# Layer 0 attention: the value product in three rounded products, with rings of three for keys, values and split weights

## The reference

```python
x = x + tanh(g_xattn[0]) * L0_xattn(layernorm(x), ctx, Wq, Wk, Wv, Wo)      # the change is here
x = x + tanh(g_ffn[0])   * L0_ffn(layernorm(x), ...)
x = x + tanh(g_xattn[1]) * L1_xattn(layernorm(x), ctx, ...)
x = x + tanh(g_ffn[1])   * L1_ffn(layernorm(x), ...)
```

```python
hidden = concatenate([context, latents], axis=1)
q, k, v = latents @ Wq.T, hidden @ Wk.T, hidden @ Wv.T
attn = softmax(q @ k.T / sqrt(96))          # per head, 100 x 461
out  = attn @ v                             # 100 x 96 per head: "the value product"
return out @ Wo.T
```

## Time and profile before

| what | value |
|---|---|
| median of 3 runs | 2783.17 us (2781.26 to 2789.91) |
| the profiled execution | 2777.63 us, span 2775.8 us |
| PE busy | 2517.4 us, 91% of the span |
| DVE / ACT / POOL busy | 52% / 30% / 19% |
| mean granted clock of TensorE | 0.949 |
| attention of layer 0 | from about 843 to 1337 us of the span |

### The profile page before, as it was taken

One profiled execution on the slowest core, in us unless ns is written; L12 is line 12 of the kernel. 1 busy time (PEld: TensorE's weight loads), 2 busy tenths in 40 slices (PEclk: granted clock), 3 DMA queues, 4 the chain that ended last, 5 costly groups with the idle time before them and its releaser, 6 DMA issues. The chain is left out here.

```text
span 2775.8 us, 32483 instructions
## 1 busy us (share of the span) xinstructions
PE 2517.4 (91%) x12384; PEld 2109.7 (76%) x12384; DVE 1455.6 (52%) x2473; ACT 827.3 (30%) x1922; POOL 533.8 (19%) x414
## 2 busy tenths in 40 slices
PE   8999999799996899998769689999999999998824
PEld 6888888589995677776569468888888888886723
DVE  6222222223102576667543546666666766766697
ACT  3222222223212333333210234333333333332323
POOL 3000000000002122211021143334334334331120
PEclk9999999899997999999989889999999999999766
DMA  6222222253222222222021113323323223322001
GB/s 197 69 69 69 69 69 62 74 173 105 68 90 85 62 79 88 80 70 61 12 69 39 55 58 95 103 84 102 101 85 103 95 90 103 93 78 75 9 0 48
DMA packets 159357, 217.40 MB, mean 78 GB/s; under 512 B 31511, under 2 KB 124083, under 8 KB 158179
## 3 DMA queue, kind: packets, MB, share of 16 engines
q1 hardware_dynamic: 159202, 215.33, 25.4%
HBM read 176.99 MB, written 38.29 MB: 78 GB/s over the span
## 5 line engine op out<-in xcount | busy, mean ns | idle before, releaser
L1034 POOL TENSOR_TENSOR attend_w_hi<-attend_w_raw,attend_one 128x1024 fp32r<-128x1024 f32 (+1 forms) x184 | 335.9, 1840 | 478.6 <-DMA attend_w_raw<-in_wo 284.6
L1326 PE MATMUL attend_ps_score<-attend_k_in,attend_q 128*100 128x361 f32 (+1 forms) x768 | 298.1, 512 | 18.6 <-ACT attend_p L1078 11.0
L1271 PE MATMUL attend_ps_gemm<-normed_hi,attend_w_hi 128*128 128x400 f32 x704 | 268.3, 381 | 39.0 <-DVE attend_w_lo L1156 39.0
L1271 PE MATMUL attend_ps_gemm<-attend_o_hi,attend_w_hi 128*128 128x400 f32 x704 | 274.0, 389 | 27.0 <-DVE attend_w_lo L1156 24.5
L1156 DVE TENSOR_TENSOR attend_w_lo<-attend_w_raw,attend_w_hi 128x1024 fp32r<-128x1024 f32 (+1 forms) x184 | 216.7, 1212 | 155.8 <-POOL attend_w_hi L1034 154.8
L1081 ACT ACTIVATE attend_p<-attend_p,attend_neg_max 100x361 f32<-100x361 f32 x256 | 150.8, 590 | 398.0 <-DVE attend_neg_max L1181 398.0
L1271 PE MATMUL attend_ps_gemm<-attend_o_hi,attend_w_lo 128*128 128x400 f32 x704 | 244.7, 348 | 0.0
L1271 PE MATMUL attend_ps_gemm<-normed_lo,attend_w_hi 128*128 128x400 f32 x704 | 244.4, 347 | 0.0
L1271 PE MATMUL attend_ps_gemm<-attend_o_lo,attend_w_hi 128*128 128x400 f32 x704 | 244.2, 347 | 0.0
L1271 PE MATMUL attend_ps_gemm<-normed_hi,attend_w_lo 128*128 128x400 f32 x704 | 243.5, 346 | 0.0
L1211 DVE SCALAR_TENSOR_TENSOR stream_tokens<-attend_ps_gemm,attend_gate,stream_tokens 128x400 f32<-128x400 f32 x192 | 121.4, 633 | 230.3 <-PE attend_ps_gemm L1271 229.7
(11 more groups left out here) (252 smaller groups left out, 5071.4 us busy)
## 6 DMA issues: line engine op xcount, KB each, us to landing
attend_w_raw<-in_wq SPq DMA_DIRECT2D x88, 512.0 KB, 3.8
attend_w_raw<-in_wo SPq DMA_DIRECT2D x64, 512.0 KB, 5.1
attend_w_raw<-in_wo SPq DMA_DIRECT2D x32, 384.0 KB, 3.5
context_ctx_raw<-in_ctxT SPq DMA_DIRECT2D x8, 1456.0 KB
attend_k_in<-scratch_k SPq DMA_DIRECT2D x64, 180.5 KB
context_ctx_raw<-in_ctxF SPq DMA_DIRECT2D x22, 512.0 KB
scratch_v<-context_v_out SPq DMA_DIRECT2D x44, 256.0 KB, 2.2
scratch_k<-context_kt_out SPq DMA_DIRECT2D x44, 256.0 KB, 5.0
```

The lines of the kernel that those rows point to most:

```text
L1034: pool.tensor_tensor(hi, w_flat(w_raw, j % RAW, j), one[:hi.shape[0]].to_broadcast(hi.shape), ALU.mult).then_inc(w_hi_done, 1)
L1271: mm = pe.matmul(out, left[a](c), right[b](c), start=(c == 0 and a == b == 0), stop=(c == chunks - 1 and a == 1))
L1326: pe.matmul(ps_score[:S, h % 2, :NK], q[:, i % 2, h, k * S:(k + 1) * S], k_in[:, u % KV_SLOTS], start=True, stop=True).then_inc(s_done, 1)
```

## The change

In layer 0 the value product is computed as three rounded products. For that `v_hi` and `v_lo` are made by GpSimd, `pt_hi` by ScalarE from `ps_turn`, and `pt_lo` by VectorE from `ps_turn` and `pt_hi`, for all four chunks. The rings of keys and values and of split weights have three buffers in layer 0 in place of four (3 + layer). Layer 1 is as before.

```diff
-    RAW, SPLIT = 3, 4
-    P_SLOTS, KV_SLOTS = 3, 4
+    RAW, SPLIT = 3, 3 + layer
+    P_SLOTS, KV_SLOTS = 3, 3 + layer
...
+        if layer == 0:
+            v_hi = sb("v_hi", [KR, 2, NCH, HD], F32R)
+            v_lo = sb("v_lo", [KR, 2, NCH, HD], F32R)
+            pt_hi = sb("pt_hi", [KR, 2, NCH, HG * S], F32R)
+            pt_lo = sb("pt_lo", [KR, 2, NCH, HG * S], F32R)
+        else:
+            pt = sb("pt", [KR, 2, NCH, HG * S])
...
+            def split_values(u):
+                if layer == 1 or u >= NU:
+                    return
+                slot, done = u % 2, 2 * u
+                pool.wait_ge(kv_load[u % KV_SLOTS], (u // KV_SLOTS + 1) * 16 * KV_DMAS)
+                if u >= 2:
+                    pool.wait_ge(pv_done, u - 1)
+                for rows, kc in ((KR, slice(0, KC)), (S, slice(KC, KC + 1))):
+                    raw = v_in[:rows, u % KV_SLOTS, kc]
+                    pool.tensor_tensor(v_hi[:rows, slot, kc], raw, one[:rows].unsqueeze(2).to_broadcast(raw.shape), ALU.mult
+                                       ).then_inc(v_hi_done, 1)
+                    done += 1
+                    pool.wait_ge(v_hi_done, done)
+                    pool.tensor_tensor(v_lo[:rows, slot, kc], raw, v_hi[:rows, slot, kc].bitcast(F32), ALU.subtract
+                                       ).then_inc(v_lo_done, 1)
...
             for u in range(NU):
+                split_values(u)
                 for j in step_tiles(u + 1):
                     weights(j)
...
# ScalarE, copy_turn(u, kc)
+                if layer == 0:
+                    act.activation(pt_hi[:ROWS[kc], u % 2, kc], ps_turn[:ROWS[kc], kc % 2, :HG * S], ACT.Copy
+                                   ).then_inc(turn_hi_done, 1)
+                    return
...
                 copy_turn(u, 0)
+                if layer == 0:
+                    copy_turn(u, 1)
                 exps(u + 2, 0)
                 copy_turn(u, 2)
+                if layer == 0:
+                    copy_turn(u, 3)
...
# VectorE, copy_turn(u, kc)
+                if layer == 0:
+                    dve.wait_ge(turn_hi_done, u * NCH + kc + 1)
+                    dve.tensor_tensor(pt_lo[:ROWS[kc], u % 2, kc], ps_turn[:ROWS[kc], kc % 2, :HG * S],
+                                      pt_hi[:ROWS[kc], u % 2, kc].bitcast(F32), ALU.subtract).then_inc(turn_lo_done, 1)
+                    return
...
+                if layer == 0:
+                    copy_turn(u, 0)
                 copy_turn(u, 1)
                 maxima(u + 2, 0)
                 if u >= HB:
                     accumulate(u - HB, 0)
-                if NCH == 4:
+                if layer == 0:
+                    copy_turn(u, 2)
                     copy_turn(u, 3)
...
# TensorE, turns(u, kc) and weigh_values(u)
-                if before:
+                if layer == 0 and t >= 2:
+                    pe.wait_ge(turn_lo_done, t - 1)
+                if layer == 1 and before:
...
+                if layer == 0:
+                    pe.wait_ge(v_lo_done, 2 * u + 2)
+                    for kc in range(NCH):
+                        pe.wait_ge(turn_lo_done, u * NCH + kc + 1)
+                        n = ROWS[kc]
+                        for v, w in ((v_hi, pt_hi), (v_hi, pt_lo), (v_lo, pt_hi)):
+                            mm = pe.matmul(ps_out[:HD, :HG * S], v[:n, u % 2, kc], w[:n, u % 2, kc],
+                                           start=(kc == 0 and v is v_hi and w is pt_hi),
+                                           stop=(kc == NCH - 1 and v is v_lo))
+                    mm.then_inc(pv_done, 1)
+                    return
```

More of the change, by code:

```diff
@@ L850, in attend @@
         v_in = sb("v_in", [KR, KV_SLOTS, NCH, HD])
+        if layer == 0:
[5 more added lines that the diff above has]
+            pt = sb("pt", [KR, 2, NCH, HG * S])
         p = sb("p", [S, P_SLOTS, HG, NK])
-        pt = sb("pt", [KR, 2, NCH, HG * S])
         neg_max = sb("neg_max", [S, P_SLOTS, HG])
@@ L891, in attend @@
         turned = sem("turned")
+        turn_hi_done = sem("turn_hi_done")
+        turn_lo_done = sem("turn_lo_done")
+        v_hi_done = sem("v_hi_done")
+        v_lo_done = sem("v_lo_done")
         turn_read = [sem("turn_read_act"), sem("turn_read_dve")]
```

## The result

The changed kernel takes 2889.41 us (2887.85 to 2890.01, 4 runs), the one before 2783.76 (4 runs): ratio 1.0375 [1.0357, 1.0393], 106 us slower. The forecast was 2850. Sign and mechanism came as predicted; the size is outside the range, by 1.4 us.

The account below looks back on a forecast made before the run. TensorE was taken as the bound in layer 0's attention. Terms 32 + 22 + 4 + 1 + 1 - 6 + 13 = +67 on 2777.6 gave 2844.6; with 5.5 for the median, 2850 us, range 2815 to 2888.

Parts of the forecast that it names:

- the clock's term: TensorE's clock falls to 1.2 GHz after stalls: 1.5 us in each of 8.5 units, 13 us (0 to 35).
- Rival 2: Slower still: clock stays low through most of ten stalled units, another 2 to 3 us each, 2875 us; chance 0.13.
- Value product: On TensorE, twelve rounded matmuls of 0.18 us take 2.18 us instead of 2.70, saving 0.52 us a unit.
- C units: 12 units with queries before them, no tile in the way: load hidden, 0.52 us kept each, -6 us.
- Kind A: Units 5, 9, 13, 17, 21, no queries before: load behind query tile, scores 7.8 us late, net 6.35 each, 32 us.
- Kind B: Units 6, 10, 14, 18, 22, following kind A: scores 4.4 us late for the load, 22 us in all.
- Kind D: Units 25 to 29, no queries at all: load 2.5 us late, net +0.8 each, 4 us (0 to 10).
- First units: Some +1 us for unit 1's load, and 1 us for added copies in the four first units without output projections.
- SPLIT = 3: Three split-weight buffers: w_hi waits for matmuls three tiles back, still half a unit or more ahead of VectorE's split: nothing.
- GpSimd "nothing": GpSimd's value split, up to 2.5 us a unit, stands behind early-ready weight tiles and is wanted a unit later: no cost.
- rival 1: Slower still: added GpSimd operations meet VectorE's scaling and normalising, and subtractions fill the rest, +20, 2870 us; chance 0.12.
- rival 3: Query tile ahead of the load does not bind, load goes out at value product's end: +5, 2788 us; chance 0.05.

Follow-up runs that it names:

- e5: Changed kernel with filler matmuls on TensorE, results unread, ahead of each wait for late keys and values: 2855.03 us, 1.0263 of the kernel before.
- e4: Changed kernel, three buffers kept, keys and values loaded one unit earlier, waiting on scores and GpSimd's value split: 2785.78 us, 1.0015 of the kernel before.
- e8: The early-load kernel (e4) with GpSimd's value split moved to after VectorE's scaling of the next unit's first maxima: 2781.96 us, 1.0005 of the kernel before.
- e3: Kernel before with only the split-weight ring cut from four to three buffers in layer 0: 2786.48 us, 1.0018.
- e1: Changed kernel with four key and value buffers again, v_hi and v_lo one buffer each instead of two: 2796.55 us, 1.0055 of the kernel before.
- e7: Changed kernel with SyncE's order turned round, key and value load ahead of the query tiles: 2823.15 us, 1.0140 of the kernel before.
- e6: The early-load kernel (e4) with GpSimd's value split moved to after the first scores of the next unit: 2787.46 us, 1.0023 of the kernel before.

## Why the prediction was wrong

The step that failed is the clock's term, 13 us, "all five A, half of B and one D" at 1.5 us each. The records have 0.50 in all fifteen stalled units, and by e5 against the changed kernel it costs 1.84 to 2.4 us in each, 32 us, and 3.5 in the first units. Two things were mis-set: the count (the D units, which stall for 1.8 to 2.0 us, are at 0.50 behind the stall as well, and of the ten shorter stalls I had counted three and a half), and the length. I took a stretch of 3.3 us of rounded matmuls from the earlier trace rows; behind a stall here stand scores in float32, and in unit 13 the low level lasted 5 us into the work. Rival 2 had the direction. The 35 us measured lie in the range I gave for the term (0 to 35), but at its upper end, and then the other terms had to be below their middles, which they were not.

- Value product: right. Its rounded matmuls are 0.18 us apart and C units are 0.5 shorter, 11 units, -5.3 (-6 predicted).
- Kind A, net 6.35 a unit without the clock: e5 has 24.22 - 16.59 = 7.6, +6 us in five. The load reached the scores 5.3 us after its issue, not 4.8, and was issued 4.55 us after the turns instead of 4.19; these are 0.9 of the 1.3 us a unit, and the rest is open.
- Kind B, 4.4: e5 has 4.55. Right.
- Kind D, 0.8: e5 has 1.8, +5 us in five. Load to scores was 4.0 us, where I had 3.5 for the bytes alone: in unit 25 the transfers of the load end at 1340.82, 3.6 us after its issue, and the scores start 0.45 us after that. The 0.5 us of the shorter value product were no help either: as e4 and e8 show, it is not on the chain in these units.
- First units, 1 + 1: 8.3 with unit 30, of which 3.5 is the clock.
- SPLIT = 3, "nothing": true in the 32 units, wrong behind them. The reason given, that w_hi is half a unit or more ahead of VectorE's split, does not hold for the last four output tiles, which follow each other with no unit between them; e3 has 3.8 us there, 2.3 of waiting and 1.5 of clock. The sum had no term for this stretch, which is 6.7 us longer in the changed kernel, value product and clock included.
- GpSimd "nothing": true only behind the late loads. Without them its value split costs 0.9 us in each D unit (e4 against e8) and in e1's A units, by the collisions shown above. This is rival 1's mechanism at a price of a few microseconds.
- The tile ahead of the load (rival 3 denied that it binds): e7 shows it binding, worth 65 us with the clock's share in it.

With the sum redone on what was measured: A 38, B 23, D 9, C -5, first units 5, clock 35 gives +105, with the stage's end (6.7) and 1 us elsewhere +112.4 on the profiled execution, where the forecast had +67. Of these 45 us the clock is 22. The forecast then added 5.5 for the median, which the changed kernel does not show (its median is 0.6 under its profiled execution); that took 6 us off the miss by luck, and left 39.

What stays open: the 1 to 3 us ahead of the stage's first matmul. That the lateness of the loads by itself costs some 75 us rests on e5, whose filling may itself hold the scores up by a few tenths.

## What to carry to other kernels

A ring's depth is a lookahead: with one buffer fewer, the load is issued one whole step later, behind whatever stands in its in-order queue, so compare its issue with the consumer one step earlier, per kind of step. Where a stall is predicted on TensorE at full clock, price the lower clock for each stall, with the work that follows it, before pricing the stall's own tenths. A saving on the busiest engine counts only in steps in which that engine is the chain: here the 11 C units, and the 5 B units once their loads are in time. A term put at nothing for the steady units has to be looked at again where the loop ends.

## What the runs showed of the hardware

Three instructions of VectorE took longer where one of GpSimd lay across them: the scaling of 100x2 took 1.48 us instead of 0.17 (e6), ending at 1258.92 where GpSimd's product ended at 1258.89, the split of 128x768 took 1.85 instead of 0.96 (e4), with the end of GpSimd's product in its midst, and the normalising took 1.98 instead of 1.57 (e4, e8). VectorE's o_lo, which reads PSUM, kept its 0.83 us beside GpSimd's value split (e4). The Trainium skill ("SBUF — State Buffer", section "Who interferes with whom") has it as an exclusive lock on a shared port pair; by that rule VectorE's wait can last as long as GpSimd's whole instruction, and the trace agrees. What I had not expected is that it matters in a kernel in which GpSimd is busy 28% of the stage (the changed kernel): where in the unit its value split stands was worth 0.9 to 1.1 us in each D unit (e4 and e6 against e8).

A load of 346 KB needed 4.0 us from issue to the start of the waiting engine (unit 25), 5.3 behind a tile of 512 KB (unit 13). The fifteen stalls of 1.8 to 8.7 us on TensorE cost 1.8 to 2.4 us each in clock beside their own length (by kinds, e5 against the changed kernel).
